# Sparse feed-forward layer: the norm of the next tokens moved ahead of the 2:4 selection, three of the selection's additions moved to GpSimd

## The reference, cut to what matters

```python
def _sparsify_2to4(h):
    g = h.reshape(B, S, I // 4, 4)
    a = jnp.abs(g)
    _, idx = jax.lax.top_k(a, 2)
    pos = jnp.arange(4)
    mask = (pos == idx[..., 0:1]) | (pos == idx[..., 1:2])
    return (g * mask.astype(g.dtype)).reshape(B, S, I)
...
h = jax.nn.silu(jnp.einsum('bsh,hi->bsi', x, w_gate)) * jnp.einsum('bsh,hi->bsi', x, w_up)
h_sparse = _sparsify_2to4(h)
return jnp.einsum('bsi,ih->bsh', h_sparse, w_down)
```

## Time and profile before

| what | value |
|---|---|
| median of 3 runs | 2016.76 us (2016.55 to 2016.97) |
| profiled execution, its own time | 2011.7 us |
| its span, first to last instruction | 2009.9 us |
| busy share of the span | PE 89%, DVE 62%, ACT 56%, POOL 31% |
| sparse layer in the span | from about 1820 us to the end |

### The profile page before, as it was taken

How to read it: one execution, slowest core, us unless ns; L and a number is a source line. 1 busy time by engine, 2 the same in 40 slices (tenths; PEclk the granted TensorE clock), 3 DMA queues, 4 the chain that set the end, 5 groups by cost and what they waited for, 6 DMA issues and landing times. The chain is left out here.

```text
span 2009.9 us, 29656 instructions
## 1 busy us (share of the span) xinstructions
PE 1784.3 (89%) x8976; PEld 1334.5 (66%) x8976; DVE 1252.3 (62%) x1995; ACT 1134.9 (56%) x2075; POOL 614.7 (31%) x501
## 2 busy tenths in 40 slices
PE   5999999998999999999998997599977599957997
PEld 4777777775877777777677885355655355635887
DVE  4555555554245555655436656588866688876997
ACT  3655565554145556655542544699934699942332
POOL 2223232222022223222200110087940087951000
PEclk9999999998999999999999998799988799978999
DMA  3000000000000000000011001122200122200000
GB/s 116 17 16 16 16 16 16 0 16 2 15 17 16 0 16 16 16 16 0 1 63 43 0 0 63 45 84 92 96 21 0 45 88 90 99 17 0 11 16 16
DMA packets 19958, 61.89 MB, mean 31 GB/s; under 512 B 2305, under 2 KB 6401, under 8 KB 19137
## 3 DMA queue, kind: packets, MB, share of 16 engines
q1 hardware_dynamic: 19904, 61.21, 8.6%
HBM read 58.84 MB, written 2.36 MB: 30 GB/s over the span
## 5 line engine op out<-in xcount | busy, mean ns | idle before, releaser
L1435 POOL TENSOR_SCALAR prob<-prob,rinv 128x128 f32<-128x128 f32 (+7 forms) x256 | 202.6, 791 | 689.2 <-DVE rinv L1077 687.5
L1503 POOL TENSOR_TENSOR m_h<-m_h,m_C 128x1024 f32<-128x1024 f32 x128 | 302.3, 2364 | 232.4 <-DVE m_h L1313 230.5
L1066 DVE TENSOR_SCALAR prob<-ps 128x128 f32<-128x128 f32 (+7 forms) x256 | 192.2, 751 | 242.3 <-PE ps L414 242.2
L449 PE MATMUL ps<-pt,v_sb 128*128 128x512 f32 (+3 forms) x768 | 319.9, 509 | 21.0 <-ACT pt L795 21.0
L1313 DVE TENSOR_TENSOR_SCAN m_h<-m_y,ps 128x1024 f32<-128x1024 f32 x128 | 292.1, 2286 | 68.2 <-ACT m_y L976 35.5
L795 ACT ACTIVATE pt<-ps 128x512 f32<-128x512 f32 (+3 forms) x384 | 181.9, 489 | 183.8 <-PE ps L438 180.6
L690 PE MATMUL ps<-m_h,ident 128*128 128x512 f32 x512 | 249.6, 611 | 4.5 <-POOL m_h L1503 4.5
L787 ACT ACTIVATE prob<-prob,nmax 128x128 f32<-128x128 f32 (+7 forms) x256 | 198.1, 774 | 83.5 <-DVE nmax L1071 82.4
L1071 DVE CUSTOM_DVE_ANT_0 prob<-prob,bias 128x128 f32<-128x128 f32 (+7 forms) x256 | 194.3, 759 | 44.3 <-issue 22.5
L972 ACT ACTIVATE m_u<-m_uT,m_bT 128x256 f32<-128x256 f32 x512 | 210.7, 495 | 2.8 <-PE ps L683 2.7
L438 PE MATMUL ps<-ident,prob 128*128 128x128 f32 x1152 | 193.7, 277 | 15.0 <-POOL prob L1435 15.0
(11 more groups left out here) (193 smaller groups left out, 3071.1 us busy)
## 6 DMA issues: line engine op xcount, KB each, us to landing
m_C<-bc_dram SPq DMA_DIRECT2D x64, 512.0 KB, 3.6
wqk_raw<-wqk_in SPq DMA_DIRECT2D x16, 512.0 KB, 3.3
wv_raw<-wv_in SPq DMA_DIRECT2D x16, 256.0 KB, 3.4
x<-x_in SPq DMA_DIRECT2D x2, 1024.0 KB, 6.9
wo_sb<-wo_in SPq DMA_DIRECT2D x1, 2048.0 KB, 11.3
q_raw<-wgu_in SPq DMA_DIRECT2D x1, 2048.0 KB, 7.7
raw<-wgu_in SPq DMA_DIRECT2D x1, 2048.0 KB, 7.6
out<-x SPq DMA_DIRECT2D x8, 256.0 KB, 2.1
```

Source lines behind the costliest of these rows:

```text
L449: mm = nc.tensor.matmul(ps[:, 6 + g, r0 * P:BANK], v_sb[:, j, u * DH:(u + 1) * DH], pt[:, idx % 3, r0 * P:BANK], start=(j == 0), stop=(j = ...
L1066: nc.vector.tensor_scalar(tile, flat[:, o:o + n], CLIP, -CLIP, ALU.min, ALU.max).then_inc(s_read, 1)
L1435: nc.gpsimd.tensor_scalar(prob[:, at:at + n], prob[:, at:at + n], rinv[:, k:k + 1], 1.0, ALU.mult, ALU.mult).then_inc(norm_done, 1)
L1503: nc.gpsimd.tensor_tensor(state, state, m_C[:, v, :], ALU.mult).then_inc(hc_done, 1)
```

## The change

Two things are changed in the sparse layer, and none outside it. On DVE, `norm(p + 1)` moves from behind `sparse(p, 0)` to ahead of it. And three of the selection's additions, `t2`, `v3` and `w3`, leave DVE for a new function `wins` on POOL. POOL waits for the three comparisons (`f_step`), computes `v3`, `t2` and, when `v3` has landed, `w3`, and counts a new semaphore `f_wins`. DVE waits for `f_wins` ahead of the second half of `k12` (it reads `t2`) and ahead of the product on element 3 (it reads `w3`). DVE's own count for a body falls from 18 to 12.

```diff
                 def settle():
-                    dve.wait_ge(f_step, (p - first) * 18 + (9 * j + step[0]))
+                    dve.wait_ge(f_step, (p - first) * 12 + (6 * j + step[0]))
...
                 settle()
                 did(nc.vector.tensor_tensor(u12[:, :, :], c1[:, :, 0:2], c2[:, :, :], ALU.add))
-                did(nc.vector.tensor_tensor(t2[:, :], c1[:, :, 1], c2[:, :, 0], ALU.add))
-                did(nc.vector.tensor_tensor(v3[:, :], c1[:, :, 2], c2[:, :, 1], ALU.add))
                 settle()
                 did(nc.vector.tensor_tensor(w0[:, :], u12[:, :, 0], c3[:, :], ALU.add))
-                did(nc.vector.tensor_tensor(w3[:, :], v3[:, :], c3[:, :], ALU.add))
                 nc.vector.tensor_tensor(k12[:, :, 0], u12[:, :, 1], c1[:, :, 0], ALU.is_gt)
+                dve.wait_ge(f_wins, (p - first) * 6 + (3 * j + 2))
                 did(nc.vector.tensor_tensor(k12[:, :, 1], c1[:, :, 2], t2[:, :], ALU.is_ge))
                 settle()
                 nc.vector.scalar_tensor_tensor(h[:, :, 0], w0[:, :], 1.5, h[:, :, 0], ALU.is_ge, ALU.mult)
+                dve.wait_ge(f_wins, (p - first) * 6 + (3 * j + 3))
                 nc.vector.scalar_tensor_tensor(h[:, :, 3], w3[:, :], 1.5, h[:, :, 3], ALU.is_le, ALU.mult)
...
                 if not begin:
                     ht_lo(p - 1, 1)
+                if not end:
+                    norm(p + 1)
                 if kind:
                     sparse(p, 0)
-                if not end:
-                    norm(p + 1)
...
+            def wins(p, j):
+
+                pool.wait_ge(f_step, (p - first) * 12 + (6 * j + 3))
+                nc.gpsimd.tensor_tensor(v3[:, :], c1[:, :, 2], c2[:, :, 1], ALU.add).then_inc(f_wins, 1)
+                nc.gpsimd.tensor_tensor(t2[:, :], c1[:, :, 1], c2[:, :, 0], ALU.add).then_inc(f_wins, 1)
+                pool.wait_ge(f_wins, (p - first) * 6 + (3 * j + 1))
+                nc.gpsimd.tensor_tensor(w3[:, :], v3[:, :], c3[:, :], ALU.add).then_inc(f_wins, 1)
+
             def body(p, last):
                 if not last:
                     norm(p + 1)
+                if kind:
+                    wins(p, 0)
+                    wins(p, 1)
```

More of the change, by code:

```diff
@@ L215, in program @@
         (fw_in, fw_hi, fw_lo, f_stat, f_mv, f_eps, f_rstd, f_xn_s, f_xt, f_xt_hi, f_xt_lo, f_gu, f_silu, f_hd,
-         f_ss, f_ssp, f_inv_s, f_absd, f_step, f_sp, f_ht, f_ht_hi, f_ht_lo, f_dn, f_res, out_s) = (
+         f_ss, f_ssp, f_inv_s, f_absd, f_step, f_wins, f_sp, f_ht, f_ht_hi, f_ht_lo, f_dn, f_res, out_s) = (
             sem(n) for n in (
@@ L219, in program @@
                 "f_xt_lo", "f_gu_full", "f_silu", "f_h_done", "f_sumsq", "f_meansq", "f_inv", "f_abs",
-                "f_step", "f_sparse", "f_ht_full", "f_ht_hi", "f_ht_lo", "f_dn_full", "f_res", "out_stored"))
+                "f_step", "f_wins", "f_sparse", "f_ht_full", "f_ht_hi", "f_ht_lo", "f_dn_full", "f_res", "out_stored"))
         (mw_in, mw_hi, mw_lo, m_pad, m_in_full, m_in_read, m_tap, m_conv, m_silu, m_xc_hi, m_xc_lo, m_xd_full,
```

## The result

| | before | changed |
|---|---|---|
| median, 16 runs each | 2016.1 us (2012.3 to 2017.3) | 2021.7 us (2017.5 to 2025.5) |
| ratio, 95% interval | | 1.0031 (1.0023 to 1.0040) |
| profiled execution: span | 2009.9 us | 2020.3 us |

The changed kernel is slower, by 1.0031 x 2016.1 - 2016.1 = 6.2 us. The forecast was +13.7 us: the right side, but more than twice the size.

A forecast was written before the change was run, and what follows sets the result against it. DVE was taken to bound the sparse layer's bodies. 16 selections at 0.88 us each add 14.1 us, the norm's move takes off 0.4: +13.7 us on 2016.8 gives 2030.5 us, range 2022 to 2040.

The forecast's parts named there:

- What bounds it: Sparse layer's bodies 1 to 5: DVE is full, 20.2 us busy of 20.5, and never waits for another engine.
- The exclusion: In the selection, DVE and POOL instructions of two SBUF inputs exclude each other and take turns, even short bf16 ones.
- the place of PE's new wait: PE's wait at `f_xn` goes and one of 1.4 us comes at `f_h`.
- no exclusion: Rival: short bf16 additions overlap in the selection, product on element 0 0.48 us earlier, 2008.7 us in all; chance 0.11.
- a falling clock inside the bodies: Rival: pauses of PE waiting for the selection lower its granted clock, 2080 us; chance 0.03.
- additions of 0.48 us: Rival: exclusion holds but POOL's additions are short, 0.48 us with 0.14 hidden, 2015 us; chance 0.05.
- dearer ones: Rival: POOL's additions take 1.28 us each, +2.7 us a selection, 2060 us; chance 0.06.
- POOL's three additions: `v3`, `t2` and `w3` on POOL: 0.73 us each alone, 1.98 us together in the turns.
- DVE's 0.92: DVE's `w0` and two halves of `k12` in the turns: 0.92 us together, 0.13 of each hidden.
- T: Time from the end of `c3` to the product on element 0: 2.65 us before, forecast 3.53.
- The norm: `norm` ahead of the selection: no wait for `rstd`, nothing gained in a full DVE, 0.4 us off in the first body.
- PE's 19.4 us as the next bound: PE's busy time in a body would become the bound and cap the gain at 1.1 us a body.

The follow-up runs named there:

- memsets on POOL: The changed kernel with POOL's three additions replaced by memsets of 512 bf16 elements, which read nothing; ratio 0.9922 to the kernel before.
- without company: The changed kernel with DVE waiting for POOL's three additions ahead of `u12`, and an unused fp32 addition ahead of them on POOL; one execution 2048.4 us.

## Why the prediction was right or wrong

**What bounds it: right.** DVE fills a body before and after, and the delay of a selection shows twice in a body (2 x 0.50 = 1.00 against 0.95).

**The exclusion: right.** It holds for short bf16 additions. The turns, their alternation and the place of PE's new wait came as forecast, and with memsets on POOL the exclusion is gone. The condition was drawn too simply, as two SBUF inputs on both engines. An addition of one input on POOL waits for its turn too, though it hardly holds DVE. And the prediction counts the 4.90 us of `f_xn` as a case of it, though `f_xn` reads one tile and two values per partition; that row shows a stall, but not this one. The rivals of no exclusion, of a falling clock inside the bodies (it is 1.00 in the windows after), of additions of 0.48 us and of dearer ones are out (0.67 to 0.74 us without company).

**The size: wrong, in the term of POOL's three additions.** I took them as 1.98 us, 0.73 each with 0.07 hidden. Without company they take 0.70 on the mean, and 0.16 is hidden: 1.62 us in the turns. Of the 0.36 us too much, 0.27 come from the hidden part and 0.09 from the price. DVE's 0.92 was right (0.90). So T is 3.15 in place of 3.53, and 16 selections cost 7.9 us in place of 14.1. The hidden part was the one quantity for which I had a single row, of an instruction of 8.7 us, and a doubled one of 4.5 beside it; a difference of 0.14 between such long ones was no measurement of a tenth of a microsecond. I then took its half. The bound was drawn too low as well: 0.14 stood as the most that could be hidden, so even with all of it hidden the sum came to 10.7 us. The line through the earlier trace rows held a better value: its fixed part is 0.17 us an addition, as much as turned out to be hidden. With that hidden the three take 3 x 0.56 = 1.68 us, T is 3.23 and the sum 9.3 us. That the fixed part is what hides is likely by its size, but not shown.

**The norm: right that it costs nothing, too small where it gains.** I took off 0.4 us, for a pause on DVE in the first body. I did not see that DVE's wait for `f_abs` ahead of the first comparison (1.13 us before) takes in the whole of `f_xn`. It is 1.07 us.

**The end: not forecast.** 1.4 us less by the clock, of which the norm's move alone has 1.0 and the additions alone 0.6. The prediction had no term for it.

The terms give 7.9 - 1.07 - 1.4 = +5.4 us; the stage has +5.1, the runs +6.2 (4.6 to 8.1 by the interval of the ratio).

**PE's 19.4 us as the next bound: wrong,** without weight in the sum: with the memsets a body runs in 18.87.

## What to carry to other kernels

Moving three short additions from a full DVE to an idle POOL was no relief here, since the instructions left on DVE beside them read two SBUF inputs as the additions do: look first for a pair in the trace that overlaps, and read whether each keeps its own length. Count such a move as DVE's remaining two-input instructions plus POOL's, in one queue; here that cost 0.50 us where 0.86 was to be gained. The engine to move to was ACT, which ran `f_xn` in 1.09 us beside POOL's `dn_lo`: the norm on it took 0.65 us off each middle body, where its new place in DVE's order took off nothing, and removed a 4 us stall at the head.

When a sum hangs on how much of an instruction hides behind its wait, take the ends of instructions of the same length, or measure it; a difference of two long ones doesn't carry it.

## What was not expected of the hardware

- An addition of two inputs on POOL needs 0.14 to 0.17 us less from the moment its turn comes than alone (0.50 to 0.60 of 0.67 to 0.74 us), DVE's 256-element ones 0.12 to 0.15 less (0.27 to 0.32 of 0.42 to 0.45).
- POOL's addition of a constant to 256 bf16 elements takes 0.85 us, more than the sum of two bf16 inputs (0.67 to 0.74); the product with a scalar per partition in fp32 took 0.48.
- The same addition of a constant waits for DVE's two-input instruction to end, but holds one of DVE's for 0.04 to 0.20 us only.
- DVE's `f_xn`, which reads one fp32 tile and two values per partition, stood still behind POOL's `dn_lo` for some 4 us (4.90 us for two where two take 0.74 otherwise).
- PE's busy time for the same matmuls is 19.4 us in a body of 20.5 and 18.87 in one of 18.87.
- After the last selection PE's granted clock returns to 2.4 GHz sooner in the changed kernel than in the one before, in two traces of each; from that selection's last product to the end of the span are 12.5 and 12.4 us against 13.9 and 13.9.
